# A causal mask written into the score banks by ScalarE, and score matmuls that add to it

## The chip, the cores and the metric

The kernel runs on one core of one Trainium2 chip. The metric is the device time of one execution in microseconds (us), given as the median of several runs. TensorE does the matmuls (PE in the profile, PEld its weight loads), VectorE is DVE, ScalarE is ACT, GpSimd is POOL, and SyncE (SP) issues the DMAs. Each engine works through its own queue in order and waits on semaphores.

## The reference, cut to what matters

A pre-norm transformer layer on 16 sequences of 256 tokens and 256 channels, with 16 heads of 16:

```
x = x + attention(layernorm(x));   x = x + ffn(layernorm(x))
scores = einsum('bihd,bjhd->bhij', q, k) * scale
mask   = idx[None, :] - idx[:, None] > WINDOW // 2        # key more than 16 ahead of the query
attn   = softmax(where(mask, -inf, scores));  out = einsum('bhij,bjhd->bihd', attn, v) @ wo.T
ffn    = (silu(x @ gate.T) * (x @ up.T)) @ down.T         # gate, up, down from 1D spline points
```

## The kernel before

One sequence is one turn t. Its work is cut into named steps, and one list, STEPS, holds all steps of all turns in one order: each step has a due time in a table (START, OWN for turns 0 to 3, 14 and 15, TURN for the others), a turn's times are shifted by 33.75 per turn, and the list is sorted by them. Every engine walks the same list and issues its part of each step, so that this list fixes the order on each engine. TURN places step s1 n at 8.294 + 3.12 n and step sc n at 42.064 + 3.12 n. The second less 33.75 is 8.314 + 3.12 n: in the list, s1 n of turn t+1 stands directly ahead of sc n of turn t, and other steps follow until the next two.

The heads are handled in eight pairs n, and the scores are computed twice:

- Step **s1** (L763 to L773): TensorE makes queries by keys of two heads with four matmuls (L770) into a pair of PSUM banks, 400 columns in each of two banks. VectorE takes the row maxima of it (L655, two reductions). Nothing else reads these scores.
- Step **mt**: the maxima are turned and stored by DMA as one more row of the query tile.
- Step **sc** (L787 to L796): TensorE makes keys by queries with that row (L794) into a pair of banks. ScalarE takes the exponential of it (L559, 800 elements in each partition), and GpSimd sets the masked part to 0. Step **av** multiplies with the values.

The causal mask enters only the maxima of s1. In turns 0 to 2 (EARLY = 3) a step **mk** behind each s1 adds it with two matmuls (identity by an upper triangle UP, L779). From turn 3 on VectorE adds UP to the bank (L649), waits for itself, and then reduces.

The pairs of banks are two. The function `places` gives each s1 and sc the pair that was given out longest ago, whatever its kind. BEFORE holds for each step the step that last had its pair, and TensorE waits until that one is emptied: an s1 is emptied when its second reduction is done, an sc when its exponential is done. Four more banks, the ring, take everything else: projections (zt, qk, v, wo), the ffn (z2, ga, up, dn) and av. Step qk's ScalarE copy (L520) and VectorE difference (L593) empty its bank; of ga, ScalarE takes the tanh (L577) and VectorE the product (L692). At the start a step hot issues 26 matmuls on a constant tile (L742), ws and wj make the ffn weights (L748, L611, L614), and SyncE issues all first loads one behind the other; UP and the bf16 identity IDB come after the load of the second sequence (L439 to L441).

Of the kernel before, what the change touches and what calls it, by code (L numbers as in the profile page):

```python
# [9 lines left out]
BF16 = mybir.dt.bfloat16  # L10
ALU = mybir.AluOpType
# [8 lines left out]
EARLY = 3  # L20
# [77 lines left out]
def steps(table):  # L98
# [133 lines left out]
def all_steps():  # L232

    out = [(at, what, 0, n) for what, n, at in steps_of_start()]
    out += [(t * PERIOD + at, what, t, n) for t in range(TURNS) for what, n, at in steps_of_turn(t)]
    return [i[1:] for i in sorted(out, key=lambda i: i[0])]


STEPS = all_steps()


def count_steps():

    seen, out = {}, {}
    for what, t, n in STEPS:
        for kind in (what, "max") if what == ("mk" if t < EARLY else "s1") else (what,):
            seen[kind] = seen.get(kind, 0) + 1
            out[kind, t, n] = seen[kind]
    return out
# [13 lines left out]
PAIRS = ("s1", "sc")  # L263


def places(kinds, banks):

    at = {i: k for k, i in enumerate(STEPS)}
    free, had, bank, before = [-1] * banks, [None] * banks, {}, {}
    for k, (what, t, n) in enumerate(STEPS):  # L270
        if what in kinds and not (what == "dn" and n):
            b = min(range(banks), key=lambda i: free[i])
            assert free[b] < k, (what, t, n)
            bank[what, t, n], before[what, t, n] = b, had[b]
            had[b] = (what, t, n) if what != "hot" else None
            free[b] = at["y", t, 0] if what == "dn" else at["ws", t, n] if what == "wj" else k
    return bank, before
# [3 lines left out]
PAIR_BANK, PAIR_BEFORE = places(PAIRS, 2)  # L281
# [3 lines left out]
def build(nc, x, wqk, wv, wo, points, powers, rows, over, ident, identb, upper, out):  # L285
    ctx = ExitStack()
    with ctx:
# [7 lines left out]
        IDB = sb("IDB", [128, 128], BF16)  # L295
        UP = sb("UP", [128, 256], BF16)
# [39 lines left out]
        ident_loaded, mask_loaded, rows_loaded = map(sem, ("ident_loaded", "mask_loaded", "rows_loaded"))  # L336
# [19 lines left out]
        masked, sel_done, in_low = map(sem, ("masked", "sel_done", "in_low"))  # L356
# [5 lines left out]
        def emptied(step):  # L362
            what, t, n = step
            if what == "dn":
                return y_done, nth("y", t, 0)
            if what == "s1":
                return max_done, nth("max", t, n)
            done = {"zt": zt_low, "qk": qk_low, "v": v_done, "mt": mt_done, "av": av_done,
                    "wo": wo_done, "z2": z2_low, "ga": ga_done, "up": up_done, "sc": exp_done,
                    "wj": ws_over, "ws": ws_sum}[what]  # L370
            return done, nth(*step)
# [44 lines left out]
        def _(sp):  # L416
# [4 lines left out]
            for what, t, n in STEPS:  # L421
                if what == "raw":
# [7 lines left out]
                    for j in PIECES:  # L430
                        c = slice(j * 512, (j + 1) * 512)
                        for dst, src in ((TAP, points), (POWER, powers)):
                            sp.dma_start(dst[rows_in(j), c], src[rows_in(j), c]).then_inc(points_loaded[j], DMA)
                        if j == PIECES[0]:
                            sp.dma_start(ROWS[:], rows.rearrange("r (a p) -> r a p", a=2)).then_inc(rows_loaded, DMA)
                            query_key(1)
                        sp.dma_start(OVER[:, c], over[:, c]).then_inc(over_loaded[j], DMA)
                        if j == PIECES[1]:
                            sp.dma_start(X[1][:], tokens(x, 1)).then_inc(x_loaded[1], DMA)  # L439
                            for dst, src in ((UP, upper), (IDB, identb)):  # L440
                                sp.dma_start(dst[:], src).then_inc(mask_loaded, DMA)  # L441
                        elif j == PIECES[2]:
                            sp.dma_start(raw(2, 1), wv.rearrange("(k p) c -> p k c", p=128)).then_inc(raw_loaded[2], DMA)
# [75 lines left out]
        def _(act):  # L519
            copy = lambda dst, src: nc.scalar.activation(dst, src, ACT.Copy)  # L520

            for what, t, n in STEPS:
# [22 lines left out]
                elif what == "v":  # L545
                    act.wait_ge(filled, 1)
                    act.wait_ge(v_made, nth("v", t, 0))
                    if t >= 2:
                        act.wait_ge(av_made, nth("av", t - 2, NG - 1))
                    copy(V[:, t % 2, :, :, 0, :].rearrange("p j h c -> p (j h) c"),  # L550
                         bank(what, t, n)[:].rearrange("p (h c) -> p h c", c=DH)).then_inc(v_done, 1)
                elif what == "sc":
# [34 lines left out]
        def _(dve):  # L587
# [7 lines left out]
            for what, t, n in STEPS:  # L595
# [46 lines left out]
                elif what == ("mk" if t < EARLY else "s1"):  # L642
                    dve.wait_ge(s1_made, nth("max", t, n))
                    pr = pair("s1", t, n)
                    if t == EARLY and n == 0:
                        dve.wait_ge(mask_loaded, 2 * DMA)
                    if t >= EARLY:
                        edge = pr[:, :, AHEAD:AHEAD + 384].rearrange("p a (i j) -> p a i j", j=128)[:, :, 0:3:2, :]
                        tt(edge, edge, UP[:].rearrange("p (i j) -> p i j", i=2).unsqueeze(1).broadcast_to([128, 2, 2, 128]),  # L649
                           ALU.add).then_inc(masked, 1)  # L650
                        dve.wait_ge(masked, nth("s1", t, n) - EARLY * NP)
# [52 lines left out]
        def _(pe):  # L704
# [27 lines left out]
            for what, t, n in STEPS:  # L732
                if BEFORE.get((what, t, n)):
                    pe.wait_ge(*emptied(BEFORE[what, t, n]))
# [4 lines left out]
                elif what == "hot":  # L739
                    pe.wait_ge(cleared, 1)  # L740
                    for i in range(26):
                        mm(bk[:, 0:S], KS[:, 0, 0, 0:128], KS[:, 0, 1, :], start=True, stop=True)  # L742
                elif what in ("wj", "ws"):
# [19 lines left out]
                elif what == "s1":  # L763
# [3 lines left out]
                    for it, c, w in ((1, W0, S), (0, 0, W0)):  # L767
                        for a in range(2):
                            r = slice(STACK * a, STACK * a + STACK - 1)
                            i = mm(pr[:, a, c:c + w], QM[r, t % 2, n, it * 128:(it + 1) * 128], KS[r, t % 2, n, 0:w],  # L770
                                   start=it == 1, stop=it == 0 and t >= EARLY, skip_group_check=True)
                    if t >= EARLY:
                        i.then_inc(s1_made, 1)  # L773
                elif what == "mk":
                    if t == 0 and n == 0:
                        pe.wait_ge(mask_loaded, 2 * DMA)
                    for a in range(2):
                        edge = pair("s1", t, n)[:, a, AHEAD:AHEAD + 384].rearrange("p (i j) -> p i j", j=128)[:, 0:3:2, :]
                        i = mm(edge, IDB[:], UP[:].rearrange("p (i j) -> p i j", i=2), start=False, stop=True,  # L779
                               skip_group_check=True)  # L780
                    i.then_inc(s1_made, 1)
                elif what == "mt":
                    pe.wait_ge(max_done, nth("max", t, NP - 1))
# [92 lines left out]
```

## Time and profile before

| what | value |
|---|---|
| median of 3 runs | 591.01 us (590.68 to 593.16) |
| profiled execution, its span | 587.0 us; no time of its own is given beside the span, so the 4.0 us between span and median stand for what lies around it |
| PE busy | 573.4 us (98%), 5402 matmuls |
| DVE busy | 505.7 us (86%) |
| ACT busy | 243.3 us (41%) |
| POOL busy | 207.6 us (35%) |

Busy time is the union of the instructions of an engine. Ends of matmuls are modelled and matmuls overlap; the distance between two starts tells what one costs in a stream. In a row of the timeline, the first number is the start from the span's start and the second the duration, both in us, and x4 means four instructions merged.

### The profile page before, as it was taken

Reading aid. Unit: us, or ns where it says so; the run is one execution under the profiler, and the core shown is the slowest. Engines: PE = TensorE matmul, PEld = TensorE weight load, DVE = VectorE, ACT = ScalarE, POOL = GpSimd, SP = SyncE. Lnnn points to the kernel's source line nnn. Section 1 sums busy time; section 2 is a strip of 40 time slices with the busy share of each in tenths; the row PEclk is TensorE's granted clock in tenths of the full one; section 3 lists DMA queues with packets and bytes.
Section 4 is the critical chain, followed back from the end, with each engine's and each line's share of the span. In section 5 each row is a group of like instructions: output and inputs, shape, how many; then the busy total and the mean of one; then the engine's idle time right before and its main releaser. Section 6 shows DMA issues by size and latency. Waiting matters only on the chain.

```text
span 587.0 us, 13711 instructions
## 1 busy us (share of the span) xinstructions
PE 573.4 (98%) x5402; PEld 501.5 (85%) x5402; DVE 505.7 (86%) x1029; ACT 243.3 (41%) x369; POOL 207.6 (35%) x249
## 2 busy tenths in 40 slices
PE   7899999999999999999999999999999999999997
PEld 6466689898998988889898888989888888988997
DVE  4998999989799898999989899899998998886642
ACT  2324634443343434444434434344443444443422
POOL 4742623333241423342242324323232324333332
PEclk9789999999999999999999999999999999999999
DMA  8451421213023131111313121222212202101000
GB/s 255 123 178 52 134 74 58 90 56 110 11 72 101 56 108 49 62 57 55 108 57 109 57 75 42 67 91 74 92 56 68 69 29 74 55 21 38 1 19 20
DMA packets 44415, 42.87 MB, mean 73 GB/s; under 512 B 4544, under 2 KB 43072, under 8 KB 44352
## 3 DMA queue, kind: packets, MB, share of 16 engines
q1 hardware_dynamic: 44352, 41.99, 22.4%
q8 instruction: 44, 0.72, 0.5%
q14 instruction: 19, 0.16, 0.1%
HBM read 12.35 MB, written 4.19 MB: 28 GB/s over the span
## 4 chain that ended last, share of the span: by engine, by line
PE 88%; DVE 9%; issue 2%; POOL 1%; ACT 0%; DVEq 0%; POOLq 0%
PE ring L720 15%; PE ring L721 13%; PE ring L722 13%; PE ring L802 8%; PE ring L727 8%; PE ring L729 7%; PE ring L728 7%; PE pair L770 7%; PE pair L794 5%; DVE M L655 2%; PE ring L711 2%; DVE W L611 1%; PE ring L742 1%; PE ring L748 1%; DVE Z L634 1%
## 5 line engine op out<-in xcount | busy, mean ns | idle before, releaser
L559 ACT ACTIVATE P<-pair 128x800 f32<-128x800 f32 x128 | 106.2, 836 | 131.1 <-PE pair L794 130.6
L720 PE MATMUL ring<-YT,WGUh 128*128 128x256 f32 x512 | 151.7, 296 | 0.0
L722 PE MATMUL ring<-YT,WGUl 128*128 128x256 f32 x512 | 144.5, 282 | 0.0
L721 PE MATMUL ring<-YT,WGUh 128*128 128x256 f32 x512 | 144.3, 282 | 0.0
L655 DVE TENSOR_REDUCE M<-pair 128x2 f32<-128x288 f32 (+1 forms) x256 | 134.3, 569 | 4.2 <-PE pair L779 0.6
L515 POOL TENSOR_TENSOR IN<-GU,IN 128x512 fp32r<-128x512 f32 x64 | 82.4, 1287 | 133.0 <-ACT IN L520 132.8
L720 PEld LDWEIGHTS ring<-YT,WGUh 128*128 128x128 f32 x512 | 96.5, 188 | 6.7 <-issue 2.2
L721 PEld LDWEIGHTS ring<-YT,WGUh 128*128 128x128 f32 x512 | 96.6, 189 | 0.0
L507 POOL TENSOR_SCALAR_AFFINE_SELECT P<-P 128x448 f32<-128x448 f32 x64 | 37.9, 592 | 165.5 <-ACT P L559 165.5
L722 PEld LDWEIGHTS ring<-YT,WGUl 128*128 128x128 f32 x512 | 96.3, 188 | 0.0
L649 DVE TENSOR_TENSOR pair<-pair,UP 128x512 f32<-128x512 f32 x104 | 71.4, 686 | 7.8 <-PE pair L770 7.6
L727 PE MATMUL ring<-WD,IN 128*128 128x256 f32 x256 | 75.5, 295 | 0.1
L728 PE MATMUL ring<-WD,IN 128*128 128x256 f32 x256 | 71.5, 279 | 0.0
L729 PE MATMUL ring<-WD,IN 128*128 128x256 f32 x256 | 71.5, 279 | 0.0
L577 ACT ACTIVATE GU<-ring 128x512 f32<-128x512 f32 x64 | 38.2, 597 | 56.7 <-PE ring L722 54.2
L692 DVE SCALAR_TENSOR_TENSOR GU<-GU,ring 128x512 f32<-128x512 f32 x64 | 43.4, 678 | 19.3 <-ACT GU L577 18.9
L770 PEld LDWEIGHTS pair<-KS,QM 63*128 63x128 f32 x512 | 38.0, 185 | 24.5 <-issue 10.9
L770 PE MATMUL pair<-KS,QM 63*128 63x256 f32 (+1 forms) x512 | 56.6, 301 | 1.8 <-DVE M L655 1.8
L520 ACT ACTIVATE IN<-GU 128x512 fp32r<-128x512 f32 x64 | 40.1, 628 | 41.4 <-DVE GU L697 41.4
L802 PE MATMUL ring<-P,V 128*32 128x256 f32 (+1 forms) x1024 | 56.0, 338 | 0.2 <-issue 0.2
L794 PE MATMUL pair<-QM,KS 64*128 64x256 f32 (+1 forms) x512 | 51.1, 282 | 1.2 <-DVE M L655 1.2
L727 PEld LDWEIGHTS ring<-WD,IN 128*128 128x128 f32 x256 | 48.2, 188 | 2.7 <-issue 0.5
(80 smaller groups left out, 1071.0 us busy)
## 6 DMA issues: line engine op xcount, KB each, us to landing
QM<-QK SPq DMA_DIRECT2D x96, 128.0 KB, 2.1
KS<-QK SPq DMA_DIRECT2D x96, 128.0 KB, 2.1
X<-x SPq DMA_DIRECT2D x32, 256.0 KB, 3.0
out<-X SPq DMA_DIRECT2D x16, 256.0 KB, 2.3
OVER<-over SPq DMA_DIRECT2D x4, 256.0 KB, 6.7
P<-wqk SPq DMA_DIRECT2D x2, 256.0 KB, 4.8
TAP<-points SPq DMA_DIRECT2D x2, 256.0 KB, 4.7
POWER<-powers SPq DMA_DIRECT2D x2, 256.0 KB, 5.7
```

The lines of the kernel that those rows point to most:

```text
L515: nc.gpsimd.tensor_tensor(IN[:, 2 * n:2 * n + 2, 1, :], halves(GU[:, n % 2, :]), IN[:, 2 * n:2 * n + 2, 0, :].bitcast(F32), ALU.subtract). ...
L559: nc.scalar.activation(P[:, g % 2, 2 * (n % 2):2 * (n % 2) + 2, :], pair(what, t, n)[:, :, 0:SW], ACT.Exp, scale=SCALE).then_inc(exp_done, 1)
L655: i = nc.vector.tensor_reduce(out=M[:, t % 2, it, :].rearrange("p (a k) -> p a k", a=2)[:, :, n], in_=pr[:, :, cols], axis=AX.X, op=ALU.ma ...
L720: mm(o, wh[:, kb, c], act[:, 0, kb, :], start=j == 0 and kb == 0, stop=False, skip_group_check=True)
L721: mm(o, wh[:, kb, c], act[:, 1, kb, :], start=False, stop=False, skip_group_check=True)
L722: i = mm(o, wl[:, kb, c], act[:, 0, kb, :], start=False, stop=False, skip_group_check=True)
L727: mm(b, act(k, 0), w[:, k, 0:D], start=first and k == 0, stop=False, skip_group_check=True)
L728: mm(b, act(k, 0), w[:, k, D:2 * D], start=False, stop=False, skip_group_check=True)
L729: i = mm(b, act(k, 1), w[:, k, 0:D], start=False, stop=False, skip_group_check=True)
L770: i = mm(pr[:, a, c:c + w], QM[r, t % 2, n, it * 128:(it + 1) * 128], KS[r, t % 2, n, 0:w], start=it == 1, stop=it == 0 and t >= EARLY, sk ...
L794: i = mm(pr[:, a, c:c + w], KS[r, t % 2, n, jt * 128:(jt + 1) * 128], QM[r, t % 2, n, S - w:S], start=jt == 0, stop=jt == 1, skip_group_ch ...
L802: i = mm(bk[32 * hl:32 * hl + 32, S - w:S], V[:, t % 2, jt, n * 4 + hl, :, :].rearrange("p a c -> p (a c)"), P[:, n % 2, hl, c:c + w], sta ...
```

## The change

Step mk, the two mask matmuls, VectorE's mask addition with its wait, UP and IDB go. A new step **sd** has ScalarE copy a bf16 tile SEED (the mask in the layout of all 400 columns, zeros where nothing is masked) into both banks of the pair that the next s1 will have. The matmuls of s1 no longer start an accumulation but add to what is there. For this every column of the banks must have been written once by TensorE, so ten of the 26 matmuls of hot go and eight new ones write the pairs.

The pairs are given out by a new function, `pair_places`: an s1 wants a pair whose last user was an sc, and an sc one whose last user was an s1. If exactly one pair fits, it is taken; else the one that was not taken last. Step sd stands in the list directly behind the step that last had the pair (the first two stand behind hot, and wait for the load of SEED). TensorE's s1 waits for sd, and sd waits until its pair is emptied.

```diff
+        if what in PAIRS:
+            want = "sc" if what == "s1" else "s1"
+            fit = [b for b in (last, 1 - last) if had[b] and had[b][0] == want]
+            b = fit[0] if len(fit) == 1 else 1 - last
+            bank[what, t, n], before[what, t, n] = b, had[b]
+            had[b], last = (what, t, n), b
...
+    before = {**pair_places(order)[1]}
+    first = [("s1",) + i[1:] for i in order if i[0] == "s1"][:2]
+    after = {before["s1", t, n]: ("sd", t, n) for what, t, n in order if what == "s1"}
+    out = []
+    for i in order:
+        out += [i, after[i]] if i in after else [i]
+        if i[0] == "hot":
+            out += [("sd",) + j[1:] for j in first]
+    return out
...
-                            for dst, src in ((UP, upper), (IDB, identb)):
-                                sp.dma_start(dst[:], src).then_inc(mask_loaded, DMA)
+                            sp.dma_start(SEED[:], seed).then_inc(seed_loaded, DMA)
...
+                elif what == "sd":
+                    if t == 0 and n == 0:
+                        act.wait_ge(seed_loaded, DMA)
+                        act.wait_ge(heated, 1)
+                    if BEFORE["s1", t, n]:
+                        act.wait_ge(*emptied(BEFORE["s1", t, n]))
+                    copy(pair("s1", t, n)[:, :, 0:SW], SEED[:].unsqueeze(1).broadcast_to([128, 2, SW])).then_inc(seeded, 1)
...
-                    if t >= EARLY:
-                        edge = pr[:, :, AHEAD:AHEAD + 384].rearrange("p a (i j) -> p a i j", j=128)[:, :, 0:3:2, :]
-                        tt(edge, edge, UP[:].rearrange("p (i j) -> p i j", i=2).unsqueeze(1).broadcast_to([128, 2, 2, 128]),
-                           ALU.add).then_inc(masked, 1)
-                        dve.wait_ge(masked, nth("s1", t, n) - EARLY * NP)
...
-                if BEFORE.get((what, t, n)):
+                if what == "s1":
+                    pe.wait_ge(seeded, nth("sd", t, n))
+                elif BEFORE.get((what, t, n)):
                     pe.wait_ge(*emptied(BEFORE[what, t, n]))
...
-                    for i in range(26):
+                    for i in range(16):
                         mm(bk[:, 0:S], KS[:, 0, 0, 0:128], KS[:, 0, 1, :], start=True, stop=True)
+                    for pr in pairs:
+                        for a in range(2):
+                            for c in (0, SW - S):
+                                i = mm(pr[:, a, c:c + S], KS[:, 0, 0, 0:128], KS[:, 0, 1, :], start=c == 0, stop=True,
+                                       skip_group_check=True)
+                    i.then_inc(heated, 1)
...
                             i = mm(pr[:, a, c:c + w], QM[r, t % 2, n, it * 128:(it + 1) * 128], KS[r, t % 2, n, 0:w],
-                                   start=it == 1, stop=it == 0 and t >= EARLY, skip_group_check=True)
...
+                                   start=False, stop=it == 0, skip_group_check=True)
```

## Rows read from the trace of the kernel before

**Rows 1.** The page, busy time, share of the span and instructions of three engines.

```profile
PE 573.4 (98%) x5402; PEld 501.5 (85%) x5402; DVE 505.7 (86%) x1029; ACT 243.3 (41%) x369; POOL 207.6 (35%) x249
...
PE 88%; DVE 9%; issue 2%; POOL 1%; ACT 0%; DVEq 0%; POOLq 0%
```

**Rows 2.** Busy time in stretches: PE, PEld, DVE, ACT, POOL, PE's granted clock, DMA share, GB/s.

```profile
20.00:26.00 6.00, 6.00 (x23) 4.00 (x20) 5.63 (x8) 1.78 (x3) 4.94 (x4) 0.54 0.37 123
...
40.00:50.00 10.00, 9.22 (x73) 5.66 (x69) 9.52 (x19) 1.99 (x4) 1.27 (x1) 1.00 0.42 133
...
50.00:60.00 10.00, 8.92 (x84) 6.26 (x82) 8.10 (x16) 6.08 (x9) 4.88 (x6) 1.00 0.21 70
...
300.00:350.00 50.00, 50.00 (x488) 44.62 (x491) 45.80 (x98) 21.24 (x32) 16.17 (x21) 1.00 0.23 74
```

**Rows 3.** Groups by line and shape: busy us, mean ns, idle before.

```profile
L559 ACT ACTIVATE P<-pair 128x800 f32<-128x800 f32 x128 | 106.2, 836 | 131.1 <-PE pair L794 130.6 <-PE ring L802 0.2
...
L655 DVE TENSOR_REDUCE M<-pair 128x2 f32<-128x512 f32 x128 | 87.3, 682 | 0.0
...
L649 DVE TENSOR_TENSOR pair<-pair,UP 128x512 f32<-128x512 f32 x104 | 71.4, 686 | 7.8 <-PE pair L770 7.6
L655 DVE TENSOR_REDUCE M<-pair 128x2 f32<-128x288 f32 x128 | 58.4, 457 | 4.2 <-PE pair L779 0.6
...
L520 ACT ACTIVATE IN<-GU 128x512 fp32r<-128x512 f32 x64 | 40.1, 628 | 41.4 <-DVE GU L697 41.4
...
L779 PE MATMUL pair<-UP,IDB 128*128 128x256 bf16 x48 | 9.1, 277 | 0.0
```

**Rows 4.** Timeline, the last s1 and sc of a steady turn.

```profile
325.21 0.30 PEld L770 LDWEIGHTS pair<-KS,QM 63*128 63x128 f32 x4 [0.23 <-issue]
325.22 0.45 PE L770 MATMUL pair<-KS,QM 63*128 63x256 f32 x4
...
325.44 0.30 PEld L794 LDWEIGHTS pair<-QM,KS 64*128 64x128 f32 x4
...
325.76 0.67 DVE L649 TENSOR_TENSOR pair<-pair,UP 128x512 f32<-128x512 f32 x1
325.83 0.19 PEld L720 LDWEIGHTS ring<-YT,WGUh 128*128 128x128 f32 x1
...
325.94 0.84 ACT L559 ACTIVATE P<-pair 128x800 f32<-128x800 f32 x1 [2.19 <-PE pair L794]
...
326.47 1.06 DVE L655 TENSOR_REDUCE M<-pair 128x2 f32<-128x288 f32 x2
```

**Rows 5.** Timeline, the same turn: the first pair and the seventh.

```profile
300.84 0.30 PEld L794 LDWEIGHTS pair<-QM,KS 64*128 64x128 f32 x4
...
301.84 1.06 DVE L655 TENSOR_REDUCE M<-pair 128x2 f32<-128x288 f32 x2
...
320.51 0.30 PEld L794 LDWEIGHTS pair<-QM,KS 64*128 64x128 f32 x4
...
321.31 0.68 DVE L593 TENSOR_TENSOR QK<-ring,QK 128x512 fp32r<-128x512 f32 x1
...
322.64 1.06 DVE L655 TENSOR_REDUCE M<-pair 128x2 f32<-128x288 f32 x2
```

**Rows 6.** DMA: SyncE's issue of UP in the timeline, and its time to landing.

```profile
7.08 0.47 SPq L441 DMA_DIRECT2D UP<-upper  x1
...
UP<-upper SPq DMA_DIRECT2D x1, 64.0 KB, 5.3
```

**Rows 7.** Timeline of the start: ACT, DVE and PE.

```profile
9.14 0.60 ACT L520 ACTIVATE ZT<-ring 128x512 fp32r<-128x512 f32 x1 [2.64 <-PE ring L711]
...
11.85 0.69 DVE L614 TENSOR_TENSOR W<-W,ring 128x512 f32<-128x512 f32 x1
...
12.59 0.39 PE L720 MATMUL ring<-ZT,WQKh 128*128 128x256 f32 x1 [0.95 <-DVE W L614]
```

**Rows 8.** Timeline, PE between 22.9 and 25.6 us, and its stream at 326 us.

```profile
24.13 0.41 PE L722 MATMUL ring<-ZT,WQKl 128*128 128x256 f32 x1
24.34 0.42 PE L720 MATMUL ring<-ZT,WQKh 128*128 128x256 f32 x1
...
326.05 0.28 PE L721 MATMUL ring<-YT,WGUh 128*128 128x256 f32 x1
326.17 0.29 PE L722 MATMUL ring<-YT,WGUl 128*128 128x256 f32 x1
```

More of the change, by code:

```diff
@@ L19 @@
 N_X1 = 4
-EARLY = 3
 AHEAD = WINDOW // 2
@@ L236, in all_steps, with pair_places, seeded_steps @@
     return [i[1:] for i in sorted(out, key=lambda i: i[0])]
-STEPS = all_steps()
+def pair_places(order):
+    had, bank, before = [None, None], {}, {}
+    last = 0
+    for what, t, n in order:
+        if what in PAIRS:
[4 more added lines that the diff above has]
+            had[b], last = (what, t, n), b
+    return bank, before
+def seeded_steps(order):
+    before = {**pair_places(order)[1]}
[7 more added lines that the diff above has]
+    return out
+PAIRS = ("s1", "sc")
+STEPS = seeded_steps(all_steps())
 def count_steps():
@@ L245, in count_steps @@
     for what, t, n in STEPS:
-        for kind in (what, "max") if what == ("mk" if t < EARLY else "s1") else (what,):
-            seen[kind] = seen.get(kind, 0) + 1
-            out[kind, t, n] = seen[kind]
+        seen[what] = seen.get(what, 0) + 1
+        out[what, t, n] = seen[what]
     return out
@@ L262 @@
 RING = ("hot", "wj", "ws", "zt", "qk", "v", "mt", "av", "wo", "z2", "ga", "up", "dn")
-PAIRS = ("s1", "sc")
 def places(kinds, banks):
@@ L280, with build @@
 RING_BANK, RING_BEFORE = places(RING, 4)
-PAIR_BANK, PAIR_BEFORE = places(PAIRS, 2)
+PAIR_BANK, PAIR_BEFORE = pair_places(STEPS)
 BEFORE = {**RING_BEFORE, **PAIR_BEFORE}
-def build(nc, x, wqk, wv, wo, points, powers, rows, over, ident, identb, upper, out):
+def build(nc, x, wqk, wv, wo, points, powers, rows, over, ident, seed, out):
     ctx = ExitStack()
@@ L294, in build @@
         ID = sb("ID", [128, 128])
-        IDB = sb("IDB", [128, 128], BF16)
-        UP = sb("UP", [128, 256], BF16)
+        SEED = sb("SEED", [128, SW], BF16)
         WQKh = sb("WQKh", [128, KB, 2 * D], F32R)
@@ L334, in build @@
         pairs = [ctx.enter_context(nc.psum_tensor(f"pair{i}", [128, 2, 512], F32)) for i in range(2)]
-        ident_loaded, mask_loaded, rows_loaded = map(sem, ("ident_loaded", "mask_loaded", "rows_loaded"))
+        ident_loaded, rows_loaded = map(sem, ("ident_loaded", "rows_loaded"))
         x_loaded = [sem(f"x_loaded{i}") for i in range(2)]
@@ L355, in build @@
             "stats_done", "mean_done", "var_done", "rstd_done", "norm_done"))
-        masked, sel_done, in_low = map(sem, ("masked", "sel_done", "in_low"))
+        heated, seed_loaded, seeded, sel_done, in_low = map(sem, ("heated", "seed_loaded", "seeded", "sel_done", "in_low"))
         N_QK, N_M = 6 * DMA, 2 * DMA
@@ L366, in emptied @@
             if what == "s1":
-                return max_done, nth("max", t, n)
+                return max_done, nth("s1", t, n)
             done = {"zt": zt_low, "qk": qk_low, "v": v_done, "mt": mt_done, "av": av_done,
@@ L641, in _ @@
                     low(QK[:, n, 1, :], bank(what, t, n)[:], QK[:, n, 0, :]).then_inc(qk_low, 1)
-                elif what == ("mk" if t < EARLY else "s1"):
-                    dve.wait_ge(s1_made, nth("max", t, n))
+                elif what == "s1":
+                    dve.wait_ge(s1_made, nth("s1", t, n))
                     pr = pair("s1", t, n)
-                    if t == EARLY and n == 0:
-                        dve.wait_ge(mask_loaded, 2 * DMA)
-                    if t >= EARLY:
-                        edge = pr[:, :, AHEAD:AHEAD + 384].rearrange("p a (i j) -> p a i j", j=128)[:, :, 0:3:2, :]
-                        tt(edge, edge, UP[:].rearrange("p (i j) -> p i j", i=2).unsqueeze(1).broadcast_to([128, 2, 2, 128]),
-                           ALU.add).then_inc(masked, 1)
-                        dve.wait_ge(masked, nth("s1", t, n) - EARLY * NP)
                     if n == 0 and t >= 2:
@@ L770, in _ @@
                             i = mm(pr[:, a, c:c + w], QM[r, t % 2, n, it * 128:(it + 1) * 128], KS[r, t % 2, n, 0:w],
-                                   start=it == 1, stop=it == 0 and t >= EARLY, skip_group_check=True)
[L772 to L780, printed above, removed]
+                                   start=False, stop=it == 0, skip_group_check=True)
                     i.then_inc(s1_made, 1)
                 elif what == "mt":
-                    pe.wait_ge(max_done, nth("max", t, NP - 1))
+                    pe.wait_ge(max_done, nth("s1", t, NP - 1))
                     for it in range(2):
@@ L864 @@
         "ident": np.eye(128, dtype=np.float32),
-        "identb": np.eye(128, dtype=ml_dtypes.bfloat16),
-        "upper": np.concatenate([upper, np.zeros((128, AHEAD)), upper[:, :J1]], axis=1).astype(ml_dtypes.bfloat16),
+        "seed": np.concatenate([np.zeros((128, AHEAD)), upper, np.zeros((128, W0)), upper[:, :J1]], axis=1).astype(ml_dtypes.bfloat16),
     }
```

30 rows, old and new, of the table OWN are left out of this document.

## The prediction

> **What bounds the kernel now.** I read the page first. TensorE is busy 98% of the span, VectorE 86%, ScalarE 41%, and the chain that ended last is 88% TensorE [rows 1]. A busy TensorE says little by itself, since ends of matmuls are modelled, so the stretches come next: from 300 to 350 us TensorE has no idle time at all, at full clock, while VectorE works 45.80 of 50 us [rows 2]. The timeline confirms it. At 325.21 an s1 begins, 0.23 us later the sc behind it, 0.39 us later the next projection [rows 4]. Nothing waits. In the steady turns any wait that TensorE gets is therefore added whole, and nothing that VectorE or ScalarE saves is seen. Only the beginning differs: from 40 to 50 us VectorE is busy 9.52 of 10 us and TensorE is not full [rows 2].
>
> **What goes.** VectorE loses 104 mask additions of 686 ns, 71.4 us [rows 3]. It isn't the bound in the steady turns, so that this is worth nothing there by itself. TensorE loses 48 mask matmuls that cover 9.1 us [rows 3], all in turns 0 to 2. Hot goes from 26 matmuls to 24, nothing.
>
> **What comes on ScalarE.** 128 seeds of 800 elements per partition. The trace has no copy of this size. The nearest row is the exponential of 800 elements, 836 ns; a copy of 512 takes 628 ns, which is the lower end [rows 3]. I take 0.84 us. The sum is 107 us, and ScalarE would be at 243 + 107 = 350 us, still far from the bound. In a steady turn a seed follows the exponential that emptied its pair, and its s1 comes a whole pair distance later, 3 us and more. So the seed itself is hidden from s1, but work queued behind it on ScalarE comes 0.9 us later.
>
> **What moves: the pairs.** This is the part that decides. Before, each s1 and sc takes the pair given out longest ago, and in a steady turn, with s1, sc, s1, sc in the list, s1 always has one pair and sc the other. An sc waits only for the exponential before it.
>
> I followed the new rule through the list. Late in turn 3 of s1 both pairs were last used by an sc. The next s1 finds two that fit and takes the one not taken last, say pair 0. Then comes sc. It wants a pair last used by an s1: only pair 0 fits, so it takes pair 0, the one that the s1 directly ahead of it has just filled. Both pairs are again last used by an sc, and the next two steps do the same with pair 1. The state keeps itself up. It holds for all 8 sc of the sequences 3 to 12, 80 in all, and for 7 more that have the distance too short in the sequences 13 and 14. In each of them TensorE must not write the sc until VectorE has reduced the s1 just made, and everything behind it on TensorE's queue (ga, up, dn, qk, av) waits too.
>
> **The price of one wait.** s1 starts at 325.21 and its last matmul ends at 325.67 [rows 4]. VectorE starts at best 0.04 us later; the two reductions take 1.06 us [rows 4]; 0.05 us for the release of TensorE makes 326.82. sc started at 325.44: the least wait is 1.38 us. Where VectorE is late, it is more. The other way to get it is from the rows of today: from the start of sc to the end of the reductions of its s1, less 0.72 us of mask (from 325.76 to 326.47), plus 0.05. That is 1.39 us for the first pair of the turn (300.84 to 302.90) and 2.52 for the seventh (320.51 to 323.70), where VectorE's difference of qk stands ahead of the reductions [rows 5] and itself waits for ScalarE. The same difference for all eight pairs of the turn, of which the first [rows 5] and the last [rows 4] stand here, gives 1.39, 1.81, 1.39, 1.39, 1.39, 2.22, 2.52 and 1.42, together 13.5 us.
>
> VectorE will be less in arrears than today, which makes some of them shorter; but a seed and an exponential now stand on ScalarE ahead of the copy of z2 and ahead of ga's tanh, whose results VectorE needs ahead of the reductions. For the fifth pair I get: sc begins, exponential to +1.33, seed to +2.2, copy of z2 to +2.85, difference to +3.6, reductions to +4.66, next sc at +4.7, where its s1 began at +2.4. That is a wait of 2.1 instead of 1.4. The sixth gives 2.1 in the same way, the seventh 2.3. Together 14.0 us per turn.
>
> **The start.** The first two seeds stand behind hot on ScalarE and wait for SEED. UP, in its place in the queue, was issued at 7.08 and took 5.3 us to land [rows 6]: about 12.4. Until then ScalarE does nothing, though it had copied the first weights at 5.9 and ZT at 9.14 [rows 7]. Two seeds (to 14.1), the weights (14.7), ZT (15.3), VectorE's difference (16.0), then its ws additions, of which the one that ended at 12.54 releases the first qk at 12.59 [rows 7]: it now ends near 17.4. So the start slips by 4.9 us, and VectorE, nearly full from there on, does not win it back. If SEED lands earlier than UP did, or slack behind it takes it up, it is 0.
>
> **Turns 0 to 2.** Here the price isn't in one row. For: up to 9.1 us of mask matmuls. Against: 15 seeds wait for the reductions of an s1 in the same pair, with all of ScalarE's queue behind them (copies of qk, v and zt, which VectorE and TensorE need next), and each puts 0.9 us into the cycle of its pair. At the bound, 15 x 0.9 = 14 us more. VectorE is full in this stretch [rows 2], so the mask matmuls beside it were mostly hidden. I take +4, with -9 and +14 as ends.
>
> **Sum.** 587.0 (the profiled span) + 10 turns x 14.0 + 7 x 1.45 (late pairs) + 4.9 + 4 = 746; with the 4.0 us between the span and the median it is 750 us. The profile gives no time for its own execution beside the span, so this 4.0 also holds whatever separates it from the median.
>
> **The clock.** TensorE's work will stop for 1.4 to 2.5 us and go on for 2 to 8 us. From 50 to 60 us it was idle for 1.08 of 10 us and the granted clock stayed 1.00; from 20 to 26 us it was 0.54 [rows 2], after a stretch of narrow matmuls with waits, and matmuls of 256 columns started 0.21 us apart instead of 0.12 [rows 8]. No row shows stops of 2 us in a dense stream, so both are open: at full clock the sum stands. If the lower level (1.2 GHz) held for 2 us of work behind each of 87 waits, it would add 87 x 2 x (0.21/0.12 - 1) = 130 us. The Trainium skill has a section for this, "A second HAM failure mode: psum-queue depth-cycling" on its page TensorE: Matmul & The Clock Gate: short idle times between groups of matmuls, from cycling through PSUM, can be enough for the clock to swing between its two levels. By that rule it would be the 880 us of the case below; the trace neither bears it out nor excludes it.
>
> **Rivals and chances.**
> - The forecast: one wait per pair behind the reductions, 735 to 765 us. 0.70.
> - The same waits at their floor, VectorE never late: 80 x 1.38 + 7 x 1.38 = 120 us, and the start hidden: 591 + 120 = 711, up to 735. For it: VectorE has 71 us less to do and more time. 0.13.
> - ScalarE's queue: the seeds' 0.9 us come through at further places (ga's tanh, ic, v), three or so per turn at 0.5: 16 x 1.5 = 24 us more, 765 to 785. 0.10.
> - The clock falls behind the waits: up to 880. 0.04.
> - Not slower: the waits of the sc are absorbed, because VectorE's work ahead of the reductions is done and TensorE's order leaves room. Then 9.1 us of mask matmuls stay as the gain, less the start: 591 - 9.1 + 4.9 = 587. It decides at a wait of about 0.05 us per sc, where the least is 1.38 by the rows. It would need the two steps in different pairs. 0.02.
> - Somewhere between, 600 to 711, because fewer sc share the pair with their neighbour than I counted: 0.01.
>
> Range: 715 to 785. A difference of 0.5%, 3 us, is what a measurement can tell here. Faster 0.02, same 0.01, slower 0.97.
>
> **What would show it.** The waits view of the changed kernel should have TensorE's L794 group waiting for VectorE's reductions, about 87 times, 1.4 to 2.5 us each, some 150 us in all. TensorE's busy share falls to about 78%, VectorE's to about 58%. The seeds should be near 0.84 us each, and the first seed should start near 12.4 us. I am wrong if L794 starts 0.2 us behind L770 in the steady turns, if the seeds take well over a microsecond, or if the granted clock leaves 1.00 after 100 us.

## The result, and the profile after

The changed kernel takes 799.75 us (798.71 to 808.19, 4 runs) against 590.85 us of the kernel before on the same chip: 1.356 times as long, 95% interval 1.348 to 1.364. The range of the prediction, 715 to 785, did not hold it. The sign, the place and the size of the waits came out; the clock did not, and the first turns cost three times what they were given. Ratios leave out one execution, of the four of e1_apart below, which took 1062.86 us where the others took 634.

The page of the kernel after, the lines that answer to [rows 1]:

```profile
PE 644.9 (81%) x5352; PEld 556.8 (70%) x5352; DVE 440.1 (55%) x925; ACT 349.8 (44%) x497; POOL 206.7 (26%) x249
...
PE 53%; DVE 26%; ACT 11%; issue 8%; SPq 1%; DMA 1%; POOL 0%; DVEq 0%; ACTq 0%
```

The chain, 88% TensorE before, now passes through VectorE for 26% and through ScalarE for 11%. The waits view names it (engine, what, whom it waited for: us in total, times, longest):

```profile
PEld pair L810 <- DVE M L672: 140.9, 90, 3.0
PE pair L810 <- DVE M L672: 126.3, 87, 2.9
```

L810 is the matmul of sc, L672 the reduction of s1's maxima. Some ninety times TensorE stands still for it (a step's weight loads and its matmuls are counted apart). The timeline of the same pair as in [rows 4]:

```profile
450.28 0.45 PE L795 MATMUL pair<-KS,QM 63*128 63x256 f32 x4
...
450.79 1.04 DVE L672 TENSOR_REDUCE M<-pair 128x2 f32<-128x288 f32 x2
451.88 0.30 PEld L810 LDWEIGHTS pair<-QM,KS 64*128 64x128 f32 x4 [1.31 <-DVE M L672]
```

From s1 to sc it is 1.60 us, where it was 0.23: the wait is 1.37, its forecast floor 1.38. The seventh pair, to be read against [rows 5], with the qk difference that comes late from ScalarE:

```profile
441.74 0.60 ACT L537 ACTIVATE QK<-ring 128x512 fp32r<-128x512 f32 x1 [2.83 <-PE ring L739]
...
442.37 0.69 DVE L617 TENSOR_TENSOR QK<-ring,QK 128x512 fp32r<-128x512 f32 x1 [1.98 <-ACT QK L537]
...
442.98 1.04 DVE L672 TENSOR_REDUCE M<-pair 128x2 f32<-128x288 f32 x2
444.08 0.30 PEld L810 LDWEIGHTS pair<-QM,KS 64*128 64x128 f32 x4 [2.15 <-DVE M L672]
```

The groups by line and shape, against [rows 3]: the seeds take what was taken for them, and VectorE now waits.

```profile
L537 ACT ACTIVATE pair<-SEED 128x800 f32<-128x800 bf16 x128 | 107.7, 842 | 19.1 <-DVE M L672 11.9 <-DMA SEED<-seed 3.0
...
L672 DVE TENSOR_REDUCE M<-pair 128x2 f32<-128x288 f32 x128 | 57.2, 447 | 36.6 <-PE pair L795 36.2
```

The start, against [rows 6] and [rows 7]: ScalarE's first copies are the two seeds, when SEED has landed, and the first qk starts at 17.77 instead of 12.59.

```profile
12.37 1.60 ACT L537 ACTIVATE pair<-SEED 128x800 f32<-128x800 bf16 x2 [3.03 <-DMA SEED<-seed]
13.90 0.61 ACT L537 ACTIVATE WQKh<-P 128x512 fp32r<-128x512 f32 x1
14.42 0.57 ACT L537 ACTIVATE ZT<-ring 128x512 fp32r<-128x512 f32 x1
...
17.77 0.58 PE L737 MATMUL ring<-ZT,WQKh 128*128 128x256 f32 x1
```

What the forecast sum lacks is in the stretches, to be read against [rows 2] (the granted clock is the number behind POOL):

```profile
300.00:350.00 50.00, 38.56 (x320) 33.65 (x319) 26.13 (x56) 19.79 (x28) 9.93 (x12) 0.90 0.15 49
350.00:400.00 50.00, 38.90 (x322) 34.17 (x320) 25.83 (x56) 20.60 (x30) 11.09 (x14) 0.90 0.15 48
```

In the steady turns the granted clock is 0.90 on average, where it was 1.00. Since it has two levels, 1.2 and 2.4 GHz, a fifth of that time is at the lower one. There matmuls of 256 columns start 0.21 us apart, as in [rows 8]:

```profile
417.34 0.42 PE L746 MATMUL ring<-WD,IN 128*128 128x256 f32 x1
417.56 0.42 PE L744 MATMUL ring<-WD,IN 128*128 128x256 f32 x1
417.77 0.41 PE L745 MATMUL ring<-WD,IN 128*128 128x256 f32 x1
```

To divide the 209.6 us between the two spans (796.6 and 587.0), I took, in both traces, the time from the start of each TensorE step to the start of the next (the mask matmuls counted with their s1) and subtracted step by step. The time ahead of an sc has grown by 148.4 us. All else has grown by 61.1: 6.4 up to the first s1, 10.8 in turns 0 to 2, and 43.9 behind them, where the steps that grew are whole projections that ran at the lower clock (one dn took 1.0 us more, one ga 1.1). How long TensorE stood idle ahead of each sc is a little less than the growth: 1.15 to 1.99 us in a steady turn, where the time from s1 to sc grew by 1.38 to 2.22.

### The profile page after: what moved, and what is told of

It is laid out like the page before. It is cut to its first block, busy times and chain, and to the rows that moved or that the text cites. A ratio compares the mean times of both kernels' runs of the same rounds, so it can differ in the third digit from the quotient of the medians.

```text
span 796.6 us, 13635 instructions
## 1 busy us (share of the span) xinstructions
PE 644.9 (81%) x5352; PEld 556.8 (70%) x5352; DVE 440.1 (55%) x925; ACT 349.8 (44%) x497; POOL 206.7 (26%) x249
## 4 chain that ended last, share of the span: by engine, by line
PE 53%; DVE 26%; ACT 11%; issue 8%; SPq 1%; DMA 1%; POOL 0%; DVEq 0%; ACTq 0%
DVE M L672 12%; PE ring L737 9%; PE ring L739 8%; PE ring L738 8%; PE pair L810 7%; PE ring L744 5%; PE ring L818 5%; PE ring L745 4%; PE ring L746 4%; ACT P L583 4%; DVE OT L684 2%; PE pair L795 2%; ACT QK L537 2%; DVE Z L692 1%; ACT GU L601 1%
## 5 line engine op out<-in xcount | busy, mean ns | idle before, releaser
L737 PE MATMUL ring<-YT,WGUh 128*128 128x256 f32 x512 | 162.3, 317 | 1.6 <-DVE YT L617 0.9
L810 PE MATMUL pair<-QM,KS 64*128 64x256 f32 (+1 forms) x512 | 58.9, 315 | 126.5 <-DVE M L672 126.3
L739 PE MATMUL ring<-YT,WGUl 128*128 128x256 f32 x512 | 154.3, 301 | 0.0
L738 PE MATMUL ring<-YT,WGUh 128*128 128x256 f32 x512 | 154.2, 301 | 0.0
L672 DVE TENSOR_REDUCE M<-pair 128x2 f32<-128x288 f32 (+1 forms) x256 | 132.8, 563 | 36.6 <-PE pair L795 36.2
L810 PEld LDWEIGHTS pair<-QM,KS 64*128 64x128 f32 x512 | 40.1, 197 | 145.6 <-DVE M L672 140.9
L537 ACT ACTIVATE pair<-SEED 128x800 f32<-128x800 bf16 x128 | 107.7, 842 | 19.1 <-DVE M L672 11.9
L737 PEld LDWEIGHTS ring<-YT,WGUh 128*128 128x128 f32 x512 | 106.3, 208 | 8.9 <-issue 2.2
L739 PEld LDWEIGHTS ring<-YT,WGUl 128*128 128x128 f32 x512 | 107.1, 209 | 0.0
L738 PEld LDWEIGHTS ring<-YT,WGUh 128*128 128x128 f32 x512 | 107.0, 209 | 0.0
L744 PE MATMUL ring<-WD,IN 128*128 128x256 f32 x256 | 79.4, 310 | 0.1
L745 PE MATMUL ring<-WD,IN 128*128 128x256 f32 x256 | 75.4, 294 | 0.0
L746 PE MATMUL ring<-WD,IN 128*128 128x256 f32 x256 | 75.2, 294 | 0.0
L714 DVE TENSOR_TENSOR GU<-GU,ring 128x512 f32<-128x512 f32 x64 | 43.8, 684 | 30.6 <-PE ring L739 28.1
L818 PE MATMUL ring<-P,V 128*32 128x256 f32 (+1 forms) x1024 | 59.2, 353 | 0.2 <-issue 0.2
```

The costliest lines, as they stand in the source:

```text
L672: i = nc.vector.tensor_reduce(out=M[:, t % 2, it, :].rearrange("p (a k) -> p a k", a=2)[:, :, n], in_=pr[:, :, cols], axis=AX.X, op=ALU.ma ...
L737: mm(o, wh[:, kb, c], act[:, 0, kb, :], start=j == 0 and kb == 0, stop=False, skip_group_check=True)
L738: mm(o, wh[:, kb, c], act[:, 1, kb, :], start=False, stop=False, skip_group_check=True)
L739: i = mm(o, wl[:, kb, c], act[:, 0, kb, :], start=False, stop=False, skip_group_check=True)
L744: mm(b, act(k, 0), w[:, k, 0:D], start=first and k == 0, stop=False, skip_group_check=True)
L745: mm(b, act(k, 0), w[:, k, D:2 * D], start=False, stop=False, skip_group_check=True)
```

## The experiments

Ten kernels follow. The diffs of e4 and e6 are against e1_apart, that of e9 is against e7_seeds_from_3, the others are against the changed kernel or the kernel before, as the text says. Each is compared with the kernel before on its own chip, which ran there at 588.6 to 589.5 us.

**e1_apart: the pair, nothing else.**

```diff
-            b = fit[0] if len(fit) == 1 else 1 - last
+            b = fit[0] if len(fit) == 1 and what == "s1" else 1 - last
```

> The changed kernel with one rule altered: an sc always takes the pair that was not given out last, so never the one that the s1 directly ahead of it has just filled. Seeds, positions of the seeds and everything else stay. Theory (the waits come from the shared pair, and the low clock from the waits): TensorE's waits of sc for the reductions, 141 us, go, the granted clock is 1.00 after the start, and what stays is the start and turns 0 to 2, some 20 us: 605 to 615 us. Rival (ScalarE's 107 us of seeds is what slows the kernel, the waits only show it): ScalarE's load is unchanged, so it stays above 700 us.

Measured: 634.35 us, 1.077 (1.070 to 1.084). The seeds are all there. The time ahead of the sc steps is 3.8 us more than before in all, and VectorE no longer stops TensorE at them. In a steady stretch the clock is back:

```profile
300.00:350.00 50.00, 48.91 (x482) 43.53 (x481) 36.84 (x86) 32.05 (x45) 16.35 (x21) 1.00 0.21 73
```

So ScalarE's load is not the cause; one rule is worth 165 us (e1_apart against the changed kernel). A steady turn is 34.36 us long against 33.79 before and 51.54 in the changed kernel; the 0.58 us lie in front of one ga, whose z2 copy stands behind a seed. But the time lies 19 us above the 605 to 615 expected. The span is 45.0 us longer than before: 23.6 up to the fourth s1 of turn 3, 7.8 from there to turn 4 with a stretch at the lower clock, 3.8 from turn 4 to turn 13, 9.8 behind that.

**e2_wait_only: the wait alone, in the kernel before.**

```diff
+                    if 3 <= t <= 12:
+                        pe.wait_ge(max_done, nth("max", t + 1, n))
```

> The kernel before with nothing but a wait added: in sequences 3 to 12 each sc waits until VectorE has reduced the s1 directly ahead of it. No seeds, pairs as before, mask by VectorE. Theory (the wait alone does it): each wait is the changed kernel's plus 0.72 us of mask, so (13.3 + 8 x 0.72) x 10 = 190 us of waits, and the granted clock falls as in the changed kernel, 40 to 60 us more: 820 to 845 us. If the clock has to do with the seeds or the new pairs and not with the waits, it stays at 1.00 and the time is about 780 us.

Measured: 890.55 us, 1.512 (1.503 to 1.521). The time ahead of the sc steps grew by 193.2 us, 19.0 in a steady turn, as expected. The rest grew by 103 instead of the 40 to 60 expected, and the time lies above the 820 to 845 of the expectation:

```profile
300.00:350.00 50.00, 37.84 (x269) 33.19 (x267) 25.09 (x51) 11.29 (x17) 8.64 (x11) 0.77 0.14 43
450.00:500.00 50.00, 35.01 (x241) 30.47 (x241) 23.47 (x46) 10.43 (x17) 7.36 (x10) 0.75 0.10 32
```

Without a seed and with the old pairs the clock falls too, and further: with eight sc per turn that come 2.2 to 3.0 us later it is at the lower level for about half the time, with eight that come 1.4 to 2.2 us later for a fifth. The waits bring it down.

**e3_warm: more matmuls, in the waits.**

```diff
+            def warm(k):
+                nxt = next(s for s in STEPS[k:] if s[0] in RING and not (s[0] == "dn" and s[2]))
...
+                    pe.wait_ge(*emptied(was))
+                for i in range(10):
+                    mm(bank(*nxt)[:, 0:S], WQKh[:, 0, 0:128], WQKh[:, 0, 0:S], start=True, stop=True)
...
+                if what == "sc" and 3 <= t <= 12:
+                    warm(k)
```

> The changed kernel with more work: ahead of the waiting sc of sequences 3 to 12 (where a ring bank is free) TensorE does ten more matmuls of 256 columns, about 1.2 us at full clock, into the ring bank that the next step overwrites. Theory (the waits set the floor, and the idle time in them lets the clock fall): the matmuls lie inside the waits and keep TensorE busy, the granted clock stays near 1.00, and the kernel gets faster by the low clock's part, 35 to 45 us: 755 to 765 us. Rival (the low clock has another cause, or costs nothing): 800 us or, where the matmuls reach beyond the wait, more.

Measured: 765.42 us, 1.299 (1.293 to 1.305): 34 us less than the changed kernel, with 800 matmuls more (against the kernel before beside it 1.299, where the changed kernel has 1.356). They lie in the wait, between s1 and sc, and in the steady stretches the clock is 1.00:

```profile
418.20 0.45 PE L807 MATMUL pair<-KS,QM 63*128 63x256 f32 x4
418.58 1.46 PE L757 MATMUL ring<-WQKh 128*128 128x256 f32 x10
...
419.11 1.02 DVE L672 TENSOR_REDUCE M<-pair 128x2 f32<-128x288 f32 x2
...
420.18 0.45 PE L822 MATMUL pair<-QM,KS 64*128 64x256 f32 x4
```

```profile
300.00:350.00 50.00, 48.68 (x431) 42.87 (x430) 27.12 (x62) 22.69 (x32) 11.10 (x14) 1.00 0.16 54
```

The sc still comes 1.98 us behind its s1, as in the changed kernel. The division by steps says more than the time does: behind the first turns, all that isn't ahead of an sc has grown by 3.1 us over the kernel before, where the changed kernel has 43.9. The time ahead of the sc is 6.3 us longer than there, because in half of the pairs the ten matmuls reach 0.16 us beyond the wait. So the clock's part is a part of its own, on top of the waits, and some 41 of the 43.9 us is it.

**e5_no_mask: nothing in the mask's place.** The maxima are taken over unmasked scores; the exponentials are masked as before.

```diff
-EARLY = 3
+EARLY = 0
...
-STEPS = all_steps()
+STEPS = [i for i in all_steps() if i[0] != "mk"]
...
-                        tt(edge, edge, UP[:].rearrange("p (i j) -> p i j", i=2).unsqueeze(1).broadcast_to([128, 2, 2, 128]),
-                           ALU.add).then_inc(masked, 1)
```

> The kernel before without any mask in the maxima: the mask matmuls and VectorE's mask additions are left out (the softmax still masks after the exponential). It is the ceiling of what the change could give, since nothing is put in their place. Theory (TensorE bounds the steady turns, VectorE's saving is worth nothing there): only mask matmuls and some waits at the beginning go, 6 to 14 us: 577 to 585 us. Rival (VectorE's 71 us are worth something in the steady turns too): below 570 us.

Measured: 591.85 us, 1.0045 (1.0012 to 1.0078). VectorE has 443.1 us instead of 505.7, and no step of a steady turn has moved by 0.02 us. The expectation, 577 to 585 us, missed: leaving out the mask matmuls was to be worth 6 us or more and brought nothing. Without them the lower clock appears in turns 0 to 2, for one stretch from 43 to 57 us; the two rows are to be read against the same stretches in [rows 2], at 1.00:

```profile
40.00:50.00 10.00, 8.24 (x48) 6.08 (x46) 8.22 (x18) 1.71 (x3) 1.27 (x1) 0.67 0.35 111
50.00:60.00 10.00, 10.00 (x60) 7.60 (x56) 6.15 (x10) 4.72 (x7) 2.46 (x3) 0.65 0.07 24
```

From 50 to 60 us TensorE now has no idle time and VectorE has. So nothing is the net of less work and a lower clock there; what the mask matmuls cost at full clock stays open. Even with nothing in the mask's place this order of steps isn't faster than before, so the change could win in it at most what this low clock hides.

**e4_late_seeds: e1_apart, the first two seeds later.**

```diff
-        if i[0] == "hot":
+        if i == ("split", 0, 2):
             out += [("sd",) + j[1:] for j in first]
```

> As e1_apart (sc never in the pair just filled, 634 us), and the first two seeds stand on ScalarE's queue behind the third weight split instead of behind hot, so that ScalarE no longer waits for the load of SEED at 12 us. Theory (that wait shifts the whole start): the first qk is back at 12.6 us from 18.6 and the end moves with it, 6 us off: 626 to 630 us. Rival (turns 0 to 2 are bound by something else and take it up): 634 us.

Measured: 623.86 us, 1.059 (1.054 to 1.063), 10.5 less than e1_apart. The first qk starts at 11.93. The first s1 is level with the kernel before (0.2 us ahead, where e1_apart was 7.2 behind). The shift of the start is thus confirmed. The time is below the 626 to 630 expected; that more came off than 6 us goes with the clock of the first 50 us, 0.81 against 0.66 in e1_apart, but no run takes the two apart.

**e6_seed_twice: e1_apart, each seed copied twice.**

```diff
+                    copy(pair("s1", t, n)[:, :, 0:SW], SEED[:].unsqueeze(1).broadcast_to([128, 2, SW])).then_inc(junked, 1)
+                    act.wait_ge(junked, nth("sd", t, n))
                     copy(pair("s1", t, n)[:, :, 0:SW], SEED[:].unsqueeze(1).broadcast_to([128, 2, SW])).then_inc(seeded, 1)
```

> As e1_apart, each seed copied twice, so that ScalarE has 108 us more (about 455 of 634 us busy). Theory (ScalarE's load costs only through its order, 0.58 us per steady turn behind one z2): a second seed costs again 0.5 to 1.5 us per steady turn and 0.9 us in each of the 15 cycles of turns 0 to 2: 655 to 680 us. Rival (ScalarE's queue is what bounds e1_apart): 100 us more, above 720.

Measured: 686.53 us, 1.164 (1.160 to 1.167), 52 more than e1_apart for 108 us of work. That is 6.5 us above the expected range and far below the rival's 720. A steady turn goes from 34.4 to about 36.0. At the first s1 of turn 4 it is 23 us further back than e1_apart. The second seed is dear where an s1 must wait for the exponential and the seed of the sc directly ahead of it: most such s1 come 2.0 us late in e1_apart and 2.9 here. Its clock in the mean was 0.932 against 0.943, so some of the 52 us may be that.

**e8_old_pairs: the seeds with the old rule for the pairs.**

```diff
-            b = fit[0] if len(fit) == 1 else 1 - last
+            b = 1 - last
```

> The changed kernel with the pairs given out as before (always the one not given out last). In a steady turn s1 then has one pair for itself, and its seed stands behind it on ScalarE and waits there for VectorE's reductions, with the exponential of the next sc behind it. Theory (only TensorE's waits are dear; ScalarE's are hidden unless something late reaches TensorE): 630 to 665 us. Rival (ScalarE's waits reach TensorE through ga's tanh and qk's copy as the sc waits did): 700 us or more.

Measured: 658.15 us, 1.116 (1.113 to 1.120), inside the expected range. A seed now waits for the reductions of the s1 that had its pair last, and the exponential behind it waits too:

```profile
ACT pair L537 <- DVE M L672: 191.2, 107, 4.2
```

This costs 4.1 us per steady turn instead of 0.6, but far less than the 17.8 of the changed kernel. In this kernel waiting for the reductions costs much less on ScalarE than on TensorE.

**e7_seeds_from_3: turns 0 to 2 as before, seeds from turn 3.** It is the kernel before with pairs as in e1_apart, a seed for each s1 from turn 3 on, and no mask addition.

```diff
-                        tt(edge, edge, UP[:].rearrange("p (i j) -> p i j", i=2).unsqueeze(1).broadcast_to([128, 2, 2, 128]),
-                           ALU.add).then_inc(masked, 1)
...
+                if what == "s1" and t >= EARLY:
+                    pe.wait_ge(seeded, nth("sd", t, n))
+                elif BEFORE.get((what, t, n)):
```

> Pairs as in e1_apart, but turns 0 to 2 keep the mask matmuls of the kernel before, and seeds replace only VectorE's mask additions from turn 3 on. Theory (e1_apart loses 23.6 us up to the fourth s1 of turn 3, 11.6 from there to turn 13 and 9.8 at the end): the first part goes, 605 to 612 us, still above the kernel before, since the seeds give TensorE nothing in the steady turns. Rival (taking 71 us from VectorE pays once the start is left alone): below 589 us.

Measured: 613.90 us, 1.042 (1.036 to 1.048). It is 2 us above the expected 605 to 612. The first part is back: the first s1 of turn 3 is 3.5 us late, where e1_apart had 23.2. Five s1 come 2.03 to 2.11 us late. They are the mirror image of the case studied here, places where the list has sc, s1 and the s1 takes the pair just filled, so that it waits for exponential and seed. The chain of this kernel, from 501 us (start, duration, what):

```profile
501.55 0.40 PE pair L820 x4
501.98 0.84 ACT P L590
502.85 0.85 ACT pair L546
503.74 0.45 PE pair L796 x4
504.19 0.45 PE ring L744
504.65 0.22 PE ring L745
504.86 0.21 PE ring L746
```

TensorE's chain goes through ScalarE twice, and behind it the projection runs at the lower clock.

**e9_never_adjacent: e7_seeds_from_3 with the rule in both orders.** Of two score steps that stand next to each other neither takes the other's pair, and a seed directly ahead of z2 stands behind it.

```diff
+    for k, (what, t, n) in enumerate(order):
...
-            b = fit[0] if len(fit) == 1 and what == "s1" else 1 - last
+            b = fit[0] if len(fit) == 1 and k > at + 1 else 1 - last
+            at = k
...
+        if out[k][0] == "sd" and out[k + 1][0] == "z2":
+            out[k], out[k + 1] = out[k + 1], out[k]
```

> As e7_seeds_from_3 (613.9 us), with two things altered: of two score steps that stand next to each other in the list neither takes the other's pair, in the order sc, s1 too, and a seed that stands directly ahead of step z2 in the list stands behind it. Theory (e7 loses 2.03 us five times, where an s1 waits for the exponential and the seed of the sc directly ahead of it, and 0.58 us per steady turn to a seed ahead of z2's copy): 10 and 5.5 us go, and some low clock with them: 593 to 600 us. Not below the kernel before, since the steady turns then are as before. Rival (something else in the seeds costs): it stays above 605 us.

Measured: 594.41 us, 1.010 (1.007 to 1.013). The five waits are gone, the steady turns are 0.2 to 0.3 us longer than before, and still the kernel is 1% slower, with VectorE at 437.1 us. Of the 6.0 us in the span, 2.9 are lost up to the fourth s1 of turn 3; why, no run shows.

**e10_before_warm: the kernel before with matmuls in the start.**

```diff
+WARM = [("ws", 0, i) for i in range(1, 6)] + [("qk", 0, 0), ("qk", 0, 1), ("qk", 1, 0), ("s1", 0, 0), ("s1", 0, 2)]
...
+                for i in range(6):
+                    mm(bank(*nxt)[:, 0:S], WQKh[:, 0, 0:128], WQKh[:, 0, 0:S], start=True, stop=True)
```

> The kernel before with work added: ten times six more matmuls of 256 columns into a free ring bank in the first 35 us, where TensorE waits and the granted clock is low for 10 us. If the low clock there is what keeps the start long, it gets faster, by at most half of the low time: 584 to 588 us. If VectorE bounds the start and the clock only follows it, it is the same or up to 5 us slower.

Measured: 589.54 us, 1.002 (0.999 to 1.004): no difference. The clock of the first 50 us is 1.00 instead of 0.90, and nothing comes of it (the kernel before first, then this one):

```profile
0.00:50.00 50.00, 42.77 (x233) 29.52 (x233) 38.96 (x75) 13.45 (x22) 24.86 (x24) 0.90 0.56 170
0.00:50.00 50.00, 46.22 (x288) 33.29 (x288) 39.29 (x75) 13.46 (x22) 24.97 (x24) 1.00 0.58 167
```

The added matmuls put the first s1 back by 2.2 us, and by the first s1 of turn 1 only 0.6 of it is left. So the low clock at the start of the kernel before isn't what keeps its start long, though a gain of a microsecond or two could hide behind what the matmuls cost. In the changed kernel's steady turns TensorE has the work that everything waits for, and there the low clock costs some 40 us. None of the ten is faster than the kernel before.

## Why the prediction was wrong in size

**Shared pairs: right.** The followed list gave 87 sc that wait behind their own neighbour; the trace has 87 to 90 such waits, and 87 sc whose own neighbour had their pair last. The price per steady turn was put at 14.0 us and is 13.28 (1.38, 1.93, 1.38, 1.38, 1.86, 1.75, 2.22, 1.38), the floor of one at 1.38 and is 1.38, the whole at 150 and is 148.4. The lengthening of the fifth and sixth by a seed ahead of z2's copy and ga's tanh was right in kind, and 0.2 and 0.35 us too long (the eight terms of the prediction add up to 13.9, not 14.0). e1_apart shows the pair to be the cause, e2_wait_only the wait to be enough.

**The start: right in cause.** 4.9 forecast, 5.2 at the first qk and 6.4 at the first s1. e4_late_seeds shows the cause.

**The seeds: right.** 842 ns each for 0.84, and hidden from s1 in the steady turns; their cost through ScalarE's queue, one of the rivals at 1.5 us per turn, is 0.58 in e1_apart.

**Turns 0 to 2: mis-sized.** The term was +4, between -9 and +14. It measured 12.7 (10.8 and 1.9 ahead of sc steps), near the upper end. The gain set against it, the mask matmuls, is nothing by e5_no_mask, the low clock that came with their absence included. e7_seeds_from_3, without seeds in these turns, shows that they and the change of the first two make the loss: its first s1 of turn 3 is 3.5 us late, where e1_apart, with the same pairs, has 23.2 and the changed kernel 18.8. How the 12.7 us divide between the seeds' 0.9 us each and the clock, which was 0.78 in the first 100 us, no run shows.

**The clock: the step that failed.** The sum was made at full clock, because from 50 to 60 us, idle for 1.08 of 10 us, it had stayed 1.00, and the fall was held to be a case of 0.04. That stretch was no model for the new one. Its idle time came in three pieces, the longest 0.51 us:

```profile
52.02 0.45 PE L770 MATMUL pair<-KS,QM 63*128 63x256 f32 x4 [0.35 <-DVE M L655]
...
58.81 0.46 PE L794 MATMUL pair<-QM,KS 64*128 64x256 f32 x4 [0.21 <-DVE M L655]
...
59.77 0.45 PE L794 MATMUL pair<-QM,KS 64*128 64x256 f32 x4 [0.51 <-DVE M L655]
```

In a steady turn of the changed kernel there are eight pieces of 1.15 to 1.99 us, 11.5 of 51.5 us. Whether their length or their share brings the clock down, the runs don't tell. The clock fell in each steady turn, which the prediction had named as a sign of being wrong. Its term was 0 and measures 43.9 us of lengthened steps, of which e3_warm gets some 41 back. The 130 us of that rival were too much: it set 1.5 us behind each of 87 waits, and 43.9 us are 0.5 us each. By the mean clock of 0.905 the lower level held for 2 x 0.095 x 796.6 = 151 us in all, a part of which was waiting. The rule cited in the prediction from the Trainium skill ("A second HAM failure mode: psum-queue depth-cycling", on the page TensorE: Matmul & The Clock Gate), that short idle times between groups of matmuls can make the clock swing, agrees with this trace (1.00 before, 0.90 after) and with e2_wait_only (0.77). Its chance should have been large, and at a size between 0 and 130 us: no case of the prediction covers 785 to 880. The terms as measured give the span: 587.0 + 136.0 for the waits of sequences 3 to 12 (140 forecast) + 10.6 for the seven late pairs (10.2) + 6.4 for the start (4.9) + 12.7 for turns 0 to 2 (4) + 43.9 for the clock (0) is 796.6.

## What to carry to other kernels

When a change alters who gets which buffer, follow the new rule through the real list of steps until it settles, and ask of each producer whether its buffer's last user stands directly ahead of it: two steps that used to overlap then wait for a third engine, and everything behind them too. When waits are put into a dense stream of matmuls, price the clock as well as the waits; filling them with throwaway matmuls tells one from the other in a single run. And work taken from an engine that isn't the bound is worth nothing: 62.6 us less on VectorE moved no step of a steady turn by 0.02 us. It is cheap to find that out first by leaving the work out.

## What was not expected of the hardware

Eight idle times of 1.15 to 1.99 us per turn of 51.5 us, with dense matmuls between them, went with a granted clock of 0.90 instead of 1.00. Where the sc came 2.2 to 3.0 us late instead of 1.4 to 2.2, eight per turn of 63 to 65 us, it was 0.77 and 0.75. Ten matmuls in each wait, together 1.46 us, held it at 1.00 in the steady turns, and the kernel with 800 matmuls more was 34 us faster.

The seed, 800 elements of bf16 copied into PSUM, took 842 ns, the exponential of as many from PSUM 837.

All seeded kernels here are written so that matmuls that don't start an accumulation add to what ScalarE wrote into the bank. That they add to it and don't overwrite it, no run shows. A seed that is overwritten would give maxima over unmasked scores, which is what e5_no_mask has, and the exponentials are masked behind the maxima in either case. The times don't depend on it. Whoever reuses the seed where its values reach the output has to test this first.
